# A graph transformer layer on one core: dst rows loaded three steps earlier, the node branch spread more evenly over the score steps, queries before edge projections, and one-hots made by three engines in the sums pass

## The reference

```python
# GNN branch, 8 heads of 32
q, k, v = xn @ Wq.T + bq, xn @ Wk.T + bk, xn @ Wv.T + bv
e = edge_attr @ We.T
k_e, v_e = k[src] + e, v[src] + e
alpha = einsum('ehc,ehc->eh', q[dst], k_e) / sqrt(32)      # scores
p = exp(alpha - segment_max(alpha, dst)[dst])
w = p / (segment_sum(p, dst)[dst] + 1e-16)
gnn = segment_sum(v_e * w, dst) + xn @ Wskip.T + bskip     # sums
# node branch: linear attention and a feed-forward block, each with a layernorm
z = 1 / (phi(q') . sum(phi(k')) + 1e-6)
x1 = layernorm(xn + (phi(q') @ (phi(k').T @ v') * z) @ Wo + bo)
mix = layernorm(x1 + relu(x1 @ W1 + b1) @ W2 + b2)
x = x + gnn + mix
# then a gated sum of 8 three-layer networks on layernorm(x)
```

## Time and profile before

| | us |
|---|---|
| median of 3 runs | 3732.03 (3723.98 to 3732.52) |
| the profiled execution, its own time | 3703.33 |
| its span in the trace | 3701.4 |
| PE busy | 3241.8 (88%) |
| DVE busy | 2927.2 (79%) |
| ACT busy | 1719.3 (46%) |
| POOL busy | 1259.3 (34%) |
| mean granted TensorE clock | 0.943 |

### The profile page before, as it was taken

The page is one execution under the profiler, slowest core; times in us unless marked ns, Lnnn a source line. Parts: engine busy times, 40 slices in busy tenths (PEclk is TensorE's granted clock), DMA queues, the critical chain, the costliest instruction groups (busy, mean ns, idle before and its releaser), DMA issues.

```text
span 3701.4 us, 72350 instructions
## 1 busy us (share of the span) xinstructions
PE 3241.8 (88%) x17312; PEld 2525.9 (68%) x17312; DVE 2927.2 (79%) x6394; ACT 1719.3 (46%) x4685; POOL 1259.3 (34%) x1313
## 2 busy tenths in 40 slices
PE   4998899999999899999999177777768999999999
PEld 3775566666666666666666145555558999999999
DVE  6776898898888888888888888888856666666665
ACT  1222333333333333333333156666646777777776
POOL 1223666666666666666664021111100000000000
PEclk9998999999999999999999599999979999999999
DMA  7336988898888988888888256666610000000000
GB/s 177 116 115 172 243 250 238 234 249 242 243 245 238 245 237 244 244 246 239 245 238 222 91 173 207 206 207 206 207 60 12 12 17 11 17 11 17 11 17 9
DMA packets 520911, 593.54 MB, mean 160 GB/s; under 512 B 187937, under 2 KB 396979, under 8 KB 520319
## 3 DMA queue, kind: packets, MB, share of 16 engines
q1 hardware_dynamic: 312408, 351.02, 32.7%
q0 software_dynamic: 201888, 232.77, 24.1%
q10 hardware_dynamic: 6409, 7.46, 0.6%
HBM read 426.91 MB, written 163.17 MB: 159 GB/s over the span
## 4 chain that ended last, share of the span: by engine, by line
PE 52%; DVE 18%; issue 13%; SPq 5%; DMA 3%; DVEq 3%; ACT 3%; ACTq 2%; another core or an unknown queue 0%
PE psum L635 10%; PE psum L637 10%; PE psum L636 10%; PE psum L713 6%; PE psum L697 5%; DMA region_s<-ab_d 3%; DVE weights L1373 3%; DVE part L1387 3%; PE psum L849 3%; PE psum L770 2%; DVE region_s L1572 2%; DVE region_x L1560 1%; ACTq L1088 1%; ACT region_s L1083 1%; DVEq L1563 1%
## 5 line engine op out<-in xcount | busy, mean ns | idle before, releaser
L600 POOL DMA_INDIRECT weights<-kv_tab,idx x450 | 547.7, 1217 | 351.9 <-ACT idx L1006 192.1
L1012 ACT ACTIVATE weights<-psum,region_s 125x250 f32<-125x250 f32 x450 | 211.7, 471 | 951.2 <-PE psum L713 524.6
L697 PE MATMUL psum<-we,weights 64*125 64x256 f32 x1800 | 578.4, 428 | 6.5 <-issue 3.4
L849 PE MATMUL psum<-region_s 125*125 125x264 f32 x1800 | 453.9, 401 | 128.8 <-DVE region_s L1572 128.8
L713 PE MATMUL psum<-region_x,weights 125*125 x1800 | 546.9, 429 | 0.0
L1129 ACT ACTIVATE region_s<-psum,bns 128x250 f32<-128x250 f32 x800 | 403.4, 555 | 287.2 <-PE psum L637 287.2
L1622 DVE TENSOR_TENSOR parts_h<-region_s,parts_h 128x500 fp32r<-128x500 f32 x400 | 269.9, 679 | 312.4 <-ACT parts_h L1133 283.1
L849 PEld LDWEIGHTS psum<-region_s 125*125 125x125 f32 x1800 | 304.6, 188 | 277.9 <-issue 152.7
L713 PEld LDWEIGHTS psum<-region_x,weights 125*125 125x125 f32 x1800 | 320.3, 198 | 190.2 <-issue 159.6
L600 POOL DMA_INDIRECT kv_more<-kv_tab,idx x300 | 364.2, 1214 | 142.6 <-issue 102.0
L697 PEld LDWEIGHTS psum<-we,weights 64*125 64x125 f32 x1800 | 291.2, 190 | 163.2 <-issue 148.0
(11 more groups left out here) (246 smaller groups left out, 7628.2 us busy)
## 6 DMA issues: line engine op xcount, KB each, us to landing
region_s<-ve_d SPq DMA_DIRECT2D x450, 256.0 KB, 2.9
ve_d<-weights SPq DMA_DIRECT2D x225, 256.0 KB
ve_d<-kv_more SPq DMA_DIRECT2D x150, 256.0 KB
weights<-in_attr_t SPq DMA_DIRECT2D x450, 62.5 KB
ve_d<-region_r SPq DMA_DIRECT2D x75, 256.0 KB
kv_tab<-region_s SPq DMA_DIRECT2D x50, 224.0 KB
region_s<-ab_d SPq DMA_DIRECT2D x450, 1.0 KB
weights<-kv_tab,idx POOLq DMA_INDIRECT x450
```

Of the source, the lines that this page charges most:

```text
L600: nc.gpsimd.indirect_dma_start(kg[r][0:T, w, :], None, kv_tab, bass.IndirectOffsetOnAxis(idx[:, r, w:w + 1], 0)).then_inc(gathered[r], 16)
L697: last = mm(psum[0:T, s % 2, w * D:(w + 1) * D], att_b[:, s % RP, w * T:(w + 1) * T], we[:, :], start=True, stop=True)
L849: last = mm(bank, hot[:, s, w, :], pv[:, s, w, 0:PV], start=(w == 0), stop=(w == 1))
```

## The change

Seven edits, five in the score pass and two in the sums pass:

1. SP loads the `dst` rows of step k + 3 in step k, ahead of the store, with a register set of its own, and so makes two register loads every six steps.
2. PE does `qprod` first in a step, then `eproj`, `spread`, `eproj`.
3. The node branch's pieces on PE are cut anew: at most three `down` products a step, the last four in steps 0 and 1 of the next block; `up` at steps 4 to 7 and 9 to 12; `attend`, `turn` and `out` one step later. ACT's and DVE's pieces that go with them move too.
4. `up` pairs 1 to 3 share PSUM bank 6, and bank 5 is left to pair 0 and `attend`, so that the wait of `up 4` for the next block's attention goes.
5. DVE's register load in the score pass comes behind `add_edges` instead of at the step's top.
6. In the sums pass the load comes behind the first product instead of at the loop's top.
7. The one-hots of the sums pass: DVE makes that of step 0 alone, ACT those of 1, 3 and 5, POOL those of 2 and 4, with two comparisons of `iota` against a number per partition.

```diff
-BY_DVE = {0: 1, 3: 2}
-BY_ACT = {1: 1, 2: 2, 4: 3, 5: 4}
+BY_DVE = {0: 1}
+BY_ACT = {1: 1, 3: 2, 5: 3}
+BY_POOL = {2: 1, 4: 2}
...
                     if s % SU == 0:
                         sp.load(regs, walk[0:1, 0, bass.ds(k, SU)])
+                        sp.load(ab_regs, walk[0:1, 0, bass.ds(k + AHEAD, SU)])
+                    if k + AHEAD < STEPS:
+                        load_ab(k + AHEAD, (s + AHEAD) % SB, ab_regs[s % SU])
                     if s >= LAGV or not (isinstance(b, int) and b == 0):
                         store_ve(k - LAGV, (s - LAGV) % SB)
...
-                    load_ab(k, s, regs[s % SU])
...
+                        order(placed)
+                        for w in range(2):
+                            compared = nc.gpsimd.tensor_scalar(hot[:, s, w, :], iota[:, :], place_in[:, s, w:w + 1], None, ALU.is_equal)
+                        compared.then_inc(hot_pool, 1)
...
-                    if n == 4 and not (isinstance(b, int) and b == NB - 1):
-                        pe.wait_ge(m_an, b + 2)
                     if o == 0 and pair >= 2:
-                        pe.wait_ge(m_hr, b * 4 + pair - 1)
+                        pe.wait_ge(m_hr, b * 4 + pair)
...
-            mix_at = {2: ("q", 0), 3: ("q", 1), 7: ("attend",), 10: ("turn",), 11: ("out", 0), 12: ("out", 1)}
...
+            mix_at = {2: ("q", 0), 3: ("q", 1), 8: ("attend",), 11: ("turn",), 12: ("out", 0), 13: ("out", 1)}
...
                     if some:
+                        qprod(k - LAGQ, (s - LAGQ) % SB, regs[s % SU])
                         eproj(k - LAGQ, (s - LAGQ) % SB, b * (SB // RP) + (s - LAGQ) // RP + 1, 0)
...
                         eproj(k - LAGQ, (s - LAGQ) % SB, b * (SB // RP) + (s - LAGQ) // RP + 1, 1)
-                        qprod(k - LAGQ, (s - LAGQ) % SB, regs[s % SU])
+                    if s in last_at and not (isinstance(b, int) and b < 2):
+                        mix(b - 2, u, last_at[s])
...
-                    if s % SU == 0:
-                        dve.load(regs, walk[0:1, 2, bass.ds(k, SU)])
...
                     add_edges(k, s, b * (SB // RK) + s // RK + 1)
+                    if s % SU == 0:
+                        dve.load(regs, walk[0:1, 2, bass.ds(k, SU)])
                     multiply(k, s)
...
-                dve.load(regs, walk[0:1, 1, bass.ds(it * SU + LAGQ - LAG, SU)])
...
+                    if s == 0:
+                        dve.load(regs, walk[0:1, 1, bass.ds(it * SU + LAGQ - LAG, SU)])
```

More of the change, by code:

```diff
@@ L58 @@
 LAGS = 2
+AHEAD = 3
 LAGP = 2
@@ L325, in build @@
         v_in = [sem(f"v_in{r}") for r in range(R)]
-        hot_dve, hot_act = sem("hot_dve"), sem("hot_act")
+        hot_dve, hot_act, hot_pool = sem("hot_dve"), sem("hot_act"), sem("hot_pool")
         place_ready, pv_ready, sum_done, acc_done = sem("place_ready"), sem("pv_ready"), sem("sum_done"), sem("acc_done")
@@ L464, in _ @@
             regs = [sp.alloc_register(f"sp_pair{s}") for s in range(SU)]
+            ab_regs = [sp.alloc_register(f"sp_ab{s}") for s in range(SU)]
             def load_ab(k, s, reg):
@@ L477, in _ @@
             load_mix(0, 0)
+            sp.load(ab_regs, walk[0:1, 0, 0:SU])
+            for s in range(AHEAD):
+                load_ab(s, s, ab_regs[s])
             sp.wait_ge(pad_in, 48)
@@ L609, in _ @@
             nc.gpsimd.memset(acc[:, NT // 2:NT, :], 0.0).then_inc(acc_zero, 1)
+            order = Order(pool, pool_o)
             def d_body(it):
-                for s in BY_ACT:
+                for s in range(SU):
+                    if s in BY_DVE:
+                        continue
                     k = it * SU + s
@@ L764, in mix @@
                         wait(pe, m_y_read, b)
-                    if n == 4 and not (isinstance(b, int) and b == NB - 1):
-                        pe.wait_ge(m_an, b + 2)
                     if o == 0 and pair >= 2:
-                        pe.wait_ge(m_hr, b * 4 + pair - 1)
+                        pe.wait_ge(m_hr, b * 4 + pair)
                     for c in range(2):
-                        last = mm(psum[:, 5 + pair % 2, o * BN:(o + 1) * BN], wm1[:, c, n * 128:(n + 1) * 128], mx1t[:, c, :],
+                        last = mm(psum[:, 5 if pair == 0 else 6, o * BN:(o + 1) * BN], wm1[:, c, n * 128:(n + 1) * 128], mx1t[:, c, :],
                                   start=(c == 0), stop=(c == 1))
@@ L785, in _ @@
             regs = [pe.alloc_register(f"pe_tile{s}") for s in range(SU)]
-            mix_at = {2: ("q", 0), 3: ("q", 1), 7: ("attend",), 10: ("turn",), 11: ("out", 0), 12: ("out", 1)}
-            late_at = {1: ("turn1",), 3: ("up", 0), 4: ("up", 1), 5: ("up", 2), 6: ("up", 3), 10: ("up", 4), 11: ("up", 5),
-                       12: ("up", 6), 13: ("up", 7), 14: ("down", 0, 3), 15: ("down", 3, 7), 16: ("down", 7, 11), 17: ("down", 11, 16)}
+            mix_at = {2: ("q", 0), 3: ("q", 1), 8: ("attend",), 11: ("turn",), 12: ("out", 0), 13: ("out", 1)}
+            late_at = {1: ("turn1",), 4: ("up", 0), 5: ("up", 1), 6: ("up", 2), 7: ("up", 3), 9: ("up", 4), 10: ("up", 5),
+                       11: ("up", 6), 12: ("up", 7), 14: ("down", 0, 3), 15: ("down", 3, 6), 16: ("down", 6, 9), 17: ("down", 9, 12)}
+            last_at = {0: ("down", 12, 14), 1: ("down", 14, 16)}
             def b_body(b, u):
@@ L811, in _ @@
             for s in range(LAGQ):
+                qprod(STEPS - LAGQ + s, SB - LAGQ + s, regs[s])
                 eproj(STEPS - LAGQ + s, SB - LAGQ + s, (STEPS - LAGQ + s) // RP + 1, 0)
@@ L815, in _ @@
                 eproj(STEPS - LAGQ + s, SB - LAGQ + s, (STEPS - LAGQ + s) // RP + 1, 1)
-                qprod(STEPS - LAGQ + s, SB - LAGQ + s, regs[s])
-            for g in late_at.values():
+                if s in last_at:
+                    mix(NB - 2, 1, last_at[s])
+            for g in (*late_at.values(), *last_at.values()):
                 mix(NB - 1, 0, g)
@@ L842, in sums @@
                     pe.wait_ge(hot_act, it * len(BY_ACT) + BY_ACT[s])
+                elif s in BY_POOL:
+                    pe.wait_ge(hot_pool, it * len(BY_POOL) + BY_POOL[s])
                 else:
@@ L1035, in mix @@
                         n = 2 * pair + o
-                        last = fn(mh[:, n, :], psum[:, 5 + pair % 2, o * BN:(o + 1) * BN], ACT.Relu,
+                        last = fn(mh[:, n, :], psum[:, 5 if pair == 0 else 6, o * BN:(o + 1) * BN], ACT.Relu,
                                   bias=cols[:, C_B1 + n:C_B1 + n + 1])
                     last.then_inc(m_hr, 1)
-            mix_at, late_at = {1: "phi", 8: "turn", 17: "turn1"}, {2: 0, 4: 1, 9: 2, 11: 3}
+            mix_at, late_at = {1: "phi", 9: "turn", 17: "turn1"}, {3: 0, 5: 1, 8: 2, 10: 3}
             def b_body(b, u):
```

12 lines of the change are left out of this document (8 added, 4 removed).

## The result

The changed kernel took **3583.72 us** (median of 4 runs, 3579.61 to 3592.31) against 3732.28 us of the kernel before, measured beside it: ratio 0.9604, interval 0.9573 to 0.9634. The forecast was 3624 us, range 3572 to 3690. At the end of the study the same kernel was measured again, beside the kernel before, and took **3519.06 us** (3515.83 to 3532.44) against 3718.65: ratio 0.948, interval 0.9441 to 0.952. The two intervals do not touch. The kernel before moved by 0.4% between the two, the changed one by 1.8%. So there are two results, and what follows says which one a reading rests on. The profiled executions took 3592.31 us (span 3590.2) and 3519.49 us (span 3517.6).

The account below looks back on a forecast made before the run. DVE was taken to bound both passes, with PE short only where pieces crowd. Score pass -45 and sums pass -62 gave -107 us, times 1.008 off 3732: 3624 us, range 3572 to 3690.

Parts of the forecast that it names:

- the 45 us: Score pass: total gain forecast, -20 us from DVE's waits for PE and -25 us from the moved load.
- the likeliest case: Whole kernel: the forecast's own case, 3624 us, with its own range of 3590 to 3665 us; chance 0.50.
- rival B: Both passes: PE's rows fall from 50 to 10, the load's 79 to 45, sums pass gains 70; 3588 us, chance 0.14.
- Sums pass, -62: Sums pass: -28 us for a one-hot off DVE, -41 for the moved load, +7 for POOL's comparisons.
- -41 for the load: Sums pass: load behind the first product, about 0.55 of 1.11 us stay, so -41 us; bounds 0 and -60.
- Rival D: Sums pass: POOL's comparisons hold up DVE's products, 135 us, from 0.38 us a comparison; 3753 us, chance 0.05.
- The load, -25: Score pass: DVE's load behind `add_edges` gets 0.3 to 0.4 us more cover on 72 loads, -25 us; bounds -60, +15.
- Waits for PE, 50 to 30, with 12 at `sum1`: Score pass: DVE's waits for PE fall from 50 to 30 us, including a new 12 us because `out` finishes later.
- a sign of being wrong altogether: Gathers or stores becoming DVE's releaser would show the forecast wrong altogether; no size given.
- DVE's floor of 1540 us: Score pass: 1669 us less 79 of load waits and 50 of PE waits leaves 1540 us, which the change does not lower.
- None of this is on DVE's path by itself: Score pass: removing PE's waits of 59, 28 and 21 us pays only as far as DVE waited for PE, 50 us.
- C, queries first makes the projections late: Score pass: projections stand 0.96 us later in PE's step, costing DVE 144 us; 3789 us, chance 0.07.

Follow-up runs that it names:

- (7): Kernel before with only the sums pass's one-hots shared among DVE, ACT and POOL, with POOL's comparisons: 3676.99 us, ratio 0.988.
- (3): Kernel before with only DVE's score-pass register load moved behind `add_edges`: 3702.59 us, ratio 0.9934.
- 11: Changed kernel with `sum1` behind the rest of step 8 and the `dst` rows loaded in their own step again: 3604.28 us, ratio 0.969.
- (2): Kernel before with only the query product put ahead of the projections in each PE step: 3707.34 us, ratio 0.9932.
- (10): Changed kernel with `sum1` behind the rest of step 8 and the query product back behind the projections: 3517.69 us, ratio 0.9462.
- Experiment 5: The kernel before, profiled again with no edit: 3714.56 us.
- the first group: Four runs with late signals, kernel before plus one change each: `dst` rows early 0.985, queries first 0.9932, score-pass load moved 0.9934, new tables and banks 1.0014.

## Why the forecast was right and where it was wrong

**Sign and mechanism: right.** Both passes are DVE's, it sheds no work in the score pass, and the gain is its waits. The clock of the score pass rose from 0.94 to 0.97 and 0.99, the wait for `ab_d` is gone, the loop of the sums pass is 6.75 us. The size was right in the traces and short in the medians: the two profiled executions differ by 111 us (forecast 107), the medians by 149 in the first measurement and 200 in the second. In the score pass the 45 us came out by luck, as shown below. The first result, 3584 us, lies outside the 3590 to 3665 of the likeliest case and beside rival B's 3588, but B's waits for PE did not fall there. (How the bounds of the terms gave 3590 to 3665 is not worked out; simply added they give 3540 to 3765.)

**Sums pass, -62: right.** -67 in the profiles; -41 for the load is 41.6 alone; -28 for the one-hot and +7 for POOL are 29.5 alone and some 4 lost where both edits meet (7). A comparison itself was mis-sized: I worked out 0.28 to 0.45 us from the earlier trace rows, and it takes 0.87. That cost next to nothing, since it takes this time on POOL:

```profile
L635 POOL TENSOR_SCALAR region_s<-iota,region_s x300: 592/936/1296, 2093.6 to 2597.5; 125x125 f32<-125x125 f32 x150
```

In the second measurement a comparison beside one of DVE's products takes 0.91 us on the mean, without one 0.60 (261 and 39 of 300). The product takes 0.698 us with a comparison beside it and 0.682 without, and that difference is the product of step 2 alone (0.74 us; 0.68 to 0.69 in the other steps, with a comparison or without). The Trainium skill ("GPSIMD Engine Reference", section 1, Specifications) says that the two engines contend where DVE's instruction has two SBUF inputs; the trace agrees, and shows who pays, POOL 0.31 us and DVE 0.016 on the mean. Rival D's comparisons of more than 0.38 us came, at 0.87, and still did not hold the products up: its mechanism is out, and not only its time.

**The load, -25: mis-sized.** It gave -66 in the first measurement (79 to 13 us) and -64 in the second (77 to 13), beyond the forecast's own bound of -60. The step that failed is "I put 0.3 to 0.4 us more cover". The cover did grow by 0.2 to 0.7 us: the engine's queued work now lasts 1.2 to 1.6 us beyond the load's start, where it was 0.9 to 1.0. But the load also became shorter, from a median of 1.93 us to 1.42:

```profile
L1487 DVEq TENSOR_LOAD <-region_s x75: 815/1423/2583, 344.2 to 1953.8; - x75
```

The load at step 12 alone, the place of the largest row (42.4 us) of the earlier trace rows, went from 2.5 to 1.4 us, and I had taken its duration for a constant. It is none, and what sets it is not shown. One lead: in the trace of before, DVE's loads beside which another engine's register load ran in their first 0.8 us took 1.97 us (median of 62), the others 0.85 (7), and PE's load overlapped 58 of 72 of DVE's before and 8 of 72 in the changed kernel. Against it: in the changed kernel the loads with no other at their start are not shorter (1.53 us, median of 27; 1.42 for the 37 with one). Moving the load alone (3) brings step 12 only to 1.96 us, so part of the 66 us most likely belongs to the other edits.

**Waits for PE, 50 to 30, with 12 at `sum1`: wrong in the first, too small in the second.** All rows counted in the same way, the profile of before has 63 us of them. In the first measurement they are 90 us in all, 58.7 of them at `sum1`, so they rose by 27. The step that failed there is the 0.5 us a block for `out`: it was 2.3, most of it by late signals (median 2.06 us). The score pass's -45 came out as -41 because one term lost what the other won, -66 + 27 = -39: a right sum of two wrong terms. In the second measurement they fell from 76 to 22, of which 14.0 at `sum1`, just what was forecast for it (12). There the pass gave 64 + 54 = 118 of its 125 us, and rival B, both waits in full, is the nearest of the cases; even B took too little, 34 and 40. The base has a part in it: the one profile of before that I read showed 63 us, another 76. The gathers, which the forecast named as a sign of being wrong altogether, did become a releaser of DVE (13.6 us in the second measurement), but a small one beside the 118 us gained.

**DVE's floor of 1540 us: too high.** The forecast took all idle time outside its two kinds of wait for short gaps. Gaps of at most 0.15 us are 47 us of the score pass in the trace of before, so its DVE work and short gaps are 1464 + 47 = 1511 us.

**"None of this is on DVE's path by itself": wrong.** The `dst` rows were worth 52 us alone and 79 in the finished kernel, and PE's waits at them 59 to 98. In this kernel PE, 93% busy and hard behind the bound engine, had no place for waits: they came back as DVE's waits for PE (8 to 101 us in 11), and the 50 us that the profile showed were no ceiling.

**C, queries first makes the projections late: wrong** as a cost in time, though DVE's waits at the projection rose from 51 to 95 us in the profile of (2); in the finished kernel the order makes no difference (10).

**The base.** The forecast carried -107 us to the median by a factor of 1.008, to -108. The profiled execution of before was 29 us below its median of 3732. Experiment 5 puts such a difference into the score pass, where the change takes waits out, so these 29 us may well have belonged to what would be saved: -107 - 29 = -136 on 3732 is 3596. That is an argument from two profiles, not a measurement.

**Open.** Why PE's signals come late and in bunches in one measurement and not in the other. Known is what it does (a score pass of 1628 us instead of 1561; `sum1` 58.7 against 14.0 us, other waits for PE 31 against 8), where it is seen (semaphore events of PE in the score pass), and that the kernel before has less of it (11% of these events against 38%). No run here tells the cause.

## What to carry to other kernels

In these traces a register load stalled its engine by its own duration less the work already queued ahead of it, and some 0.2 us (at step 12 before: 2.56 - 0.98 = 1.58 us, measured 1.77). Put it behind the longest instruction of the step, and expect its duration to change with the place too. Where two engines run within a few per cent of each other, a wait of the second can be worth its full length. What an edit is worth alone and in the finished kernel can differ: the tables gave nothing alone and 45 us in the finished kernel, the query order 22 us alone and nothing in it, though here the late signals of the first group may have a part in both. Before a variant's gain is credited to its edit, run the unedited kernel again beside it, and before a wait is read from a profile, see whether its semaphore events are complete.

## What was not expected of the hardware

- The same register load took 0.8 to 4.4 us in the trace of before. Its median fell from 1.93 to 1.58 us when it was moved alone and to 1.42 in the changed kernel.
- Semaphore events of matmuls can come late and in bunches: in the first profile of the changed kernel those of `out` stand 2.06 us (median, up to 4.8) behind the recorded end, four events of different products within 0.15 us, at a granted clock of 1.00 around them; in the second profile of the same text end and event agree within 0.02 us. Such profiles also lack about a third of these events.
- POOL's comparison of 125 x 125 in fp32 takes 0.60 us alone and 0.91 beside a product of DVE that reads two SBUF inputs; the product pays 0.016 us on the mean, all of it in one of six steps.
